# Macaron layer (MoE, attention, MoE): the place-counting matmuls moved behind the step's last expert product

## The reference

```python
logits = jnp.einsum('btd,ed->bte', x, Wr)          # 8 experts
top_vals, top_idx = jax.lax.top_k(logits, K)       # K = 2
w = jax.nn.softmax(top_vals, axis=-1)
...
pos_all = jnp.cumsum(oh, axis=1) - oh
pos = jnp.take_along_axis(pos_all, flat_e[..., None], axis=-1)[..., 0]
keep = pos < C                                     # C = 193
...
expert_out = jnp.einsum('becd,edf->becf', expert_in, We)
...
out = jnp.einsum('btk,btkd->btd', w, gathered)
```

## Time and profile before

| what | value |
|---|---|
| three runs | 935.0, 937.36, 949.56 us (median 937.36) |
| profiled execution | 934.77 us |
| its span in the profile | 933.1 us |
| busy share of the span | PE 89%, DVE 81%, ACT 69%, POOL 58% |
| picks of the first expert layer | from 16 to 158 us |
| picks of the second expert layer | from 779 to 919 us |

### The profile page before, as it was taken

One profiled execution on the slowest core, in us unless ns is written; L12 is line 12 of the kernel. 1 busy time (PEld: TensorE's weight loads), 2 busy tenths in 40 slices (PEclk: granted clock), 3 DMA queues, 4 the chain that ended last, 5 costly groups with the idle time before them and its releaser, 6 DMA issues. The chain is left out here.

```text
span 933.1 us, 23978 instructions
## 1 busy us (share of the span) xinstructions
PE 828.5 (89%) x6498; PEld 383.2 (41%) x6498; DVE 752.8 (81%) x2534; ACT 640.4 (69%) x1538; POOL 537.4 (58%) x838
## 2 busy tenths in 40 slices
PE   4999999359899999999999999999999977999997
PEld 3444444124334444444434444444444334444443
DVE  3899988348788888988988988888899416999996
ACT  3776666211687778778778778777877844766775
POOL 3677777431654654655565565475453323778787
PEclk9999999655899999999999999999999997999999
DMA  6500000042221322232232232132221001000101
GB/s 165 106 0 0 0 0 0 34 153 87 99 94 65 124 104 69 104 108 80 85 122 82 70 134 91 62 121 103 73 101 36 2 3 22 28 30 26 30 26 43
DMA packets 57044, 62.50 MB, mean 67 GB/s; under 512 B 6752, under 2 KB 50656, under 8 KB 56864
## 3 DMA queue, kind: packets, MB, share of 16 engines
q1 hardware_dynamic: 56992, 61.86, 20.5%
HBM read 32.23 MB, written 29.36 MB: 66 GB/s over the span
## 5 line engine op out<-in xcount | busy, mean ns | idle before, releaser
L1094 DVE TENSOR_REDUCE att_neg_max<-att_max 128x1 bf16<-128x512 f32 (+3 forms) x704 | 414.5, 638 | 61.8 <-PE att_max L888 59.5
L987 ACT ACTIVATE att_probs<-att_exp 128x512 f32<-128x512 f32 x640 | 357.6, 596 | 102.4 <-PE att_exp L907 98.5
L1059 POOL TENSOR_SCALAR_AFFINE_SELECT att_probs<-att_probs 128x512 f32<-128x512 f32 x256 | 159.0, 634 | 240.9 <-ACT att_probs L987 240.8
L907 PE MATMUL att_exp<-att_q_st,att_k_st 53*128 53x512 bf16 (+3 forms) x1024 | 223.0, 302 | 0.6 <-ACT att_probs L987 0.6
L885 PE MATMUL att_max<-att_k_st,att_q_st 51*128 51x384 bf16 (+2 forms) x768 | 191.2, 285 | 19.4 <-DVE att_neg_max L1094 11.4
L923 PE MATMUL att_pv<-att_probs,att_v 128*32 128x512 f32 (+3 forms) x2048 | 191.8, 448 | 2.7 <-POOL att_probs L1059 2.4
L360 ACT ACTIVATE moe_scaled<-moe_hi,moe_gates 128x128 f32<-128x128 f32 x512 | 145.7, 371 | 61.4 <-PE moe_hi L306 61.0
L520 DVE SCALAR_TENSOR_TENSOR x<-moe_lo,moe_gates,x 128x128 f32 (+1 forms) x512 | 160.7, 339 | 20.3 <-PE moe_lo L300 19.2
L888 PE MATMUL att_max<-att_k_st,att_q_st 64*128 64x128 bf16 x1024 | 176.0, 224 | 0.0
L885 PEld LDWEIGHTS att_max<-att_k_st,att_q_st 51*128 51x128 bf16 x768 | 71.1, 95 | 216.4 <-DVE att_neg_max L1094 159.1
L300 PE MATMUL moe_lo<-moe_we,moe_hT 128*128 128x512 f32 x256 | 136.0, 613 | 0.0
(11 more groups left out here) (81 smaller groups left out, 872.1 us busy)
## 6 DMA issues: line engine op xcount, KB each, us to landing
qk_parts<-att_parts SPq DMA_DIRECT2D x32, 384.0 KB, 2.7
att_q_st<-qk_parts SPq DMA_DIRECT2D x64, 192.0 KB
att_k_st<-qk_parts SPq DMA_DIRECT2D x64, 192.0 KB
qk_parts<-att_parts SPq DMA_DIRECT2D x32, 256.0 KB, 2.1
x<-in_L_attn_x SPq DMA_DIRECT2D x16, 256.0 KB, 2.9
qk_parts<-att_parts SPq DMA_DIRECT2D x32, 128.0 KB, 1.7
out<-x SPq DMA_DIRECT2D x16, 256.0 KB, 2.3
moe_we<-in_L_ffn_We SPq DMA_DIRECT2D x2, 512.0 KB, 4.9
```

Source lines behind the costliest of these rows:

```text
L907: mm = nc.tensor.matmul(exp_ps[m % RING][:, c:c + S - j * P], k_st[par][low:low + FINE_ROW, r, j * P:(j + 1) * P], q_st[par][low:low + FIN ...
L987: nc.scalar.activation(probs[g % 2][:, n, :], exp_ps[m % RING][:], ACT.Exp).then_inc(exp_done, 1)
L1059: nc.gpsimd.affine_select(out=view, in_=view, compare_op=ALU.is_ge, fill=0.0, base=0, pattern=[[0, 4], [1, P]], channel_multiplier=-1).the ...
L1094: nc.vector.tensor_reduce(neg_max[par][:, g // 2, 1 - g % 2, heads[0]:heads[0] + len(heads), i], max_ps[m % RING][:, 0:len(heads) * width] ...
```

## The change

In TensorE's `step`, the hi product of tile 3 stands in front of the places of the next sequence, not behind them. Both layers use the same function, so both change. No instruction is added or removed, and no wait is changed; the order of the two groups on TensorE is.

```diff
@@ -319,10 +319,9 @@
                         experts_lo(b, par, t)
                         experts_hi(b, par, t)
                     experts_lo(b, par, 3)
+                    experts_hi(b, par, 3)
                 if next1:
                     places(b + 1)
-                if this:
-                    experts_hi(b, par, 3)
```

## The result

The changed kernel takes 920.26 us (median of 4 runs, 915.14 to 922.57) against 936.18 us (median of 4), where 925.8 was forecast. The ratio is 0.9854, 95% interval 0.9822 to 0.9886: 1.5% faster, or about 14 us; the medians lie 15.9 us apart. Some executions of any kernel here take some 15 us longer at a lower granted clock, and the ratios leave them out (949.56 us before is one, and it lifts that median), while in `change_again`, profiled in such an execution, the steps of the expert layers are as long as in the others and the extra time lies between the layers. The profiled execution took 918.97 us with a span of 917.2 us, 15.8 and 15.9 us less than before.

A forecast was written before the change was run, and what follows sets the result against it. The prediction took a loop through two waits, picks to places and gates to logits, as the bound. 13 pairs at 0.80 us give 10.4 us off 934.8, so 924.4, plus 1.4 offset: 925.8 us, range 915.0 to 939.0.

The forecast's parts named there:

- its own case: Pairs of expert-layer steps gain 0.80 us each; 925.8 us in all, own range 922 to 930, chance 0.64.
- the rival of TensorE as the bound: All 0.77 us of TensorE's wait for picks goes in 27 steps: 915.5 us, chance 0.08.
- The wait for picks goes, the transposes come 0.92 us sooner: On TensorE, the hi product fills the wait; transposes start 0.13 us behind the places, not 1.06.
- A: One of two alternating steady steps: from the places matmuls at 835.83 to those at 845.06, 9.23 us.
- The hi product waits for nothing: On TensorE, the moved hi product finds its PSUM buffer free 1.15 us before TensorE is ready.
- Logits: On TensorE, logits wait for the gates, first matmul 0.24 us behind; 0.42 us sooner in A, 0.19 in B.
- B: The other alternating step, following the hardware loop's jump: places at 845.06 to 854.56, 9.50 us.
- First term, 0.62 in A: Earlier transposes free ACT's copy and POOL, so root, VectorE's shift and picks come 0.62 us sooner.
- Step B and the tie: Variances gain 0.15 us; VectorE's line 501 against POOL's sum adds 0.22 or loses 0.17: 0.37 or -0.02.
- The sum: A pair of steps gains 0.99 or 0.60 us, middle 0.80; 13 pairs give 10.4 us (7.8 to 12.9).
- The moved wait: Rival: TensorE stops for the gates as long as it did for picks; 935.5 us, chance 0.21.
- The collision: Rival: POOL's sum begins just before VectorE's line 501 every step, costing 0.79 us a pair; 946.5 us, chance 0.07.

The follow-up runs named there:

- change_again: The changed kernel itself once more, in more rounds, nothing else altered: 920.87 us, 0.9852 of the kernel before.
- places_late: Changed kernel with the places moved behind the first lo product of the next step: 919.16 us, 0.9849 of the kernel before.
- unroll: Changed kernel with the expert layers' hardware loop written out on TensorE and VectorE: 921.16 us, 0.9859 of the kernel before.
- turn_late: Changed kernel with the transposes moved behind the first lo product of the next step: 934.70 us, 1.0004 of the kernel before.
- scale_first_before: Kernel before, with ACT scaling tile 3 of the previous step ahead of copying the transposed tiles: 927.28 us, 0.9939 of the kernel before.
- turn_first: Kernel before, with the next sequence's transposes put ahead of the places, hi product still behind them: 926.52 us, 0.9902 of the kernel before.
- yield_gw_before: Kernel before, with POOL's sum of tile 2 held until VectorE has written its weights: 929.41 us, 0.9958 of the kernel before.

## Why the prediction was right

The direction, the mechanism and the range from 915.0 to 939.0 held. The size did not: the forecast gain was 10.4 us, the ratio gives about 14 and the profiles 15.9, and 920.3 lies below the 922 to 930 that the prediction gave its own case. By its number alone the result stands midway between this case (925.8) and the rival of TensorE as the bound (915.5); it is the rows and the runs that decide for the mechanism.

- *The wait for picks goes, the transposes come 0.92 us sooner.* Shown: from +1.11 to +0.26 us behind the picks in A, 0.85. Behind the jump only to +0.66, since TensorE is then still 0.2 us in the hi product and the jump is no longer covered (0.43 us from places to transposes, 0.10 with the loop written out). I had counted TensorE's jump as slack; `places_late`, which covers it and gains nothing, shows that it is. For VectorE's part `unroll` doesn't settle it, since the collision took there what the jump gave.
- *The hi product waits for nothing.* Shown: it follows the lo product without a gap (849.62 and 850.48, the 0.86 us of one product).
- *Logits.* The term was mis-sized. Their matmuls start 0.05 us behind the gates (845.14, 845.19) and not 0.24; the load that isn't covered shows as 0.11 us more inside the group (0.92 to the lo product in A, 0.81 in B). The lo product of tile 1 starts 0.50 us sooner in A, not 0.42.
- *First term, 0.62 in A.* Measured 0.66 in the second layer, 0.61 in the first. The chain is the one worked out: the root starts +4.37 (forecast +4.44). `turn_late` and `scale_first_before` show that it runs through ACT's copy and POOL: the one takes the gain away although the hi product fills the wait, the other gives 0.6% with TensorE's order untouched.
- *Step B and the tie.* The tie went to VectorE in every steady pair: 0.15 us at line 501, then 0.46 at the multiply, which waits for the sum's end. For this case the working gave 0.37; measured 0.38 in the second layer, 0.28 in the first. (The prediction calls the 0.60 us row A's; by its time, 845.97, it lies in B, behind the places at 845.06. The working used the right row.) The variances took 0.16, not the 0.19 counted. I took the middle of the two outcomes, 0.80 a pair; the measured 1.04 and 0.88 belong to the upper one, 0.99.
- *The sum.* The mis-sized term is the pair, 0.80: behind the first two steps and ahead of the last one, the two layers have 12 pairs, and they gave 11.5 us, 0.96 each. The sentence that failed is "the last step of each layer gains nothing of its own": between the last two picks the time went from 8.52 to 8.22 and 8.10, 0.30 and 0.42 us, because the logits in front of the last picks are sooner by half a microsecond too. (Counted from the last picks but one, the kernel issues its last output 0.55 us sooner too, so this is not only a matter of where the picks are read.) That makes the 12.2 us. The other 1.6 us in the layers lie in their first two steps and 1.6 in attention; the runs don't tie either to the change, so that the profiles' 15.9 overstate it.
- *Rivals.* The moved wait is true in a small part: TensorE does stop at the gates now in A, 0.22 us, but the loop got shorter beneath it. TensorE as the bound: not reached, it is busy 98% but still waits for gates in A and for the picks that end B. The collision exists (0.66 to 0.68 us at line 501 in `turn_first` and `unroll`, 0.5 us more than alone where 0.72 was priced), but in this change it eased, for VectorE was carried along.

What stays open is how much of B's remaining 9.1 us could go. Each attempt to free VectorE there moved its collision with POOL elsewhere; giving POOL's sums to another engine wasn't tried.

## What to carry to other kernels

When an engine idles in front of a wait, ask what stands behind the waiting instruction, not how long it idles: here the filled wait was worth nothing (`turn_late`) until the transposes came early too, since the loop ran from the picks over another engine's copy and a third engine's sums back to the picks. Find such a loop by measuring each link from one event (here +1.11, +5.04, +6.09 us behind the picks) and see which link has something in it that needn't be there. Where two engines block each other on single instructions, a gain of 0.2 us can flip the order and cost 0.5, so that removing one collision has to be followed to the next.

## What was not expected of the hardware

The order in which VectorE and POOL get through can't be read from starts that lie close: in the changed kernel POOL's sum is recorded at 852.06 and VectorE's add at 852.07, and still VectorE passes in 0.15 us. In the first layer POOL's start is recorded even 0.05 us ahead:

```profile
80.61 0.80 POOL L396 TENSOR_TENSOR moe_part<-moe_scaled 128x256 f32<-128x256 f32 x1 [0.54 <-ACT moe_scaled L359]
...
80.66 0.15 DVE L500 TENSOR_TENSOR moe_g<-moe_g,moe_first 128x32 f32<-128x32 f32 x1
```

In `unroll` POOL is ahead by 0.10 us (844.80 against 844.90) and VectorE takes 0.68.

The Trainium skill, SBUF — State Buffer, section "Who interferes with whom", names two SBUF inputs on VectorE as what contends with a reading POOL, and for a single input only VectorE's two-port modes. The runs agree for the add at line 501 (0.15 to 0.68 us), the weights' multiply (0.23 to 0.46), the shift (0.16 to 0.68) and the comparisons (0.18 to 0.53). The adds of line 520, with one input in PSUM and one in SBUF, stayed at 0.31 to 0.35 us in both kernels, whatever POOL did. But the variances, with one input in SBUF, are held up too: they take 0.34 us in step B before, ending 0.03 us behind POOL's row, and up to 0.47 in `yield_gw_before`. In which mode they run, no row shows.
